# Graph layer, edge sum: the repeated operands of the one-hots move from SBUF to two PSUM banks, in runs of 8, and the tables hold each value twice

## The chip, the core and the metric

One core of a Trainium2 chip runs the whole kernel. The metric is the device time of one execution in microseconds (us), lower is better. The kernel before takes 2285.66 us, the median of 3 runs (2284.79 to 2289.71).

## What is computed

`x` holds 6250 nodes of 256 numbers. There are 200,000 edges with random `src`, `dst` and weight; the reference sorts them by `dst`, but its graph sum reads them as a sparse matrix whose row is `src` and whose column is `dst`.

```
out = segment_sum(edge_weight[:, None] * xn[dst], src, 6250) + node_vec1      # the edge sum
x = x + out + linear_attention(xn)                                            # xn = layernorm(x)
x = x + mixture_of_8_experts_top_2(layernorm(x))
```

Only the first line, the edge sum, is touched by the change.

## The kernel before, in words

The kernel runs in stages: `front` (layer norm, keys and values), `edge_sum`, `stragglers` (edges that did not fit), `route` and `experts`. The change lies in `edge_sum`.

`edge_sum` cuts the nodes into 49 blocks of 128 and works on 7 groups of source blocks (`NG = 7`), each with all 49 target tiles: 343 **steps**, in 49 **units** of 7 steps (`BU = 7`). All of it is written out straight, engine by engine; the order on each engine is that of its function `unit`, and the engines meet through semaphores alone.

A step `t` needs the edges between one group and one tile. They lie in a **table**, one row of 23 small numbers for each of 128 slots (3 of the column `PICK`, 4 each of source, target and three parts of a weight). A step goes like this:

- DVE, `hots` (lines 1278 to 1290): it compares `ends` with the values of the slot, each repeated along the free axis, and so makes the one-hots `hot` (1408 elements of bf16). Then it multiplies the one-hots of the source by the three parts of the weight into `hot_w` (1536 elements of bf16). `picks` (line 1295) makes `pick_w` (384 elements of f32) in the same way from `hot` and the f32 weights.
- PE, `blocks` (L903): 12 matmuls of bf16 make a 128 x 512 block of weights in bank 0 or 1.
- ACT, `evacuate` (L1027) copies the block to SBUF (`stage`).
- PE, `rows` (L911, L915): 8 matmuls of f32 with the window of `xn` and 6 with the rows that POOL gathered (L817, three indirect DMAs a step into four sets of buffers).
- DVE, `add` (L1316) adds the sum to `acc`.

The repeated operands are `cur` (bf16, each value of a table row repeated `REP = 16` times) and `cur_w` (f32, likewise). ACT writes them once per unit for the 7 steps of the next unit, in `take` (L1019 and L1021), in two halves of 4 and 3 steps, into one of two buffers in turn. DVE reads each run of 16 eight times over (128 / `REP`).

In the first 42 units the engines also sort the edges of a later group, one sort a unit. PE adds 34 short matmuls `base` (L845, in the first step of a unit) and 34 of `make_table` (L854, in the last). DVE adds the instructions L1121 to L1186, the large ones 816 to 2176 elements wide. ACT adds copies that repeat operands (L973, L981, L996) and `unpack` or `unpack_list` (L1002, L1007, L1010), which move the finished column of a table from PSUM into `table[par]`. There DVE splits the bit fields in place: `part` (L1172, L1173) in one unit, `make_list` (L1180 to L1186) in the next, in turn. Eight sorts run ahead of the first step (`AHEAD`), beside the matmuls `mix` (L864) of the attention, which use the banks `mix_ps`. The last 7 units sort nothing and normalise rows for the next stage instead.

The buffers bound how far an engine runs ahead: DVE makes the one-hots of step `t + i + 2` in its iteration `i` and ends the iteration with the sum of step `t + i - 1`; PE makes the blocks of step `t + i + 1` in its iteration `i` and then the rows of `t + i`.

Of the kernel before, what the change touches and what calls it, by code (L numbers as in the profile page):

```python
# [22 lines left out]
P = 128  # L23
F32 = mybir.dt.float32
# [12 lines left out]
REP = 16  # L37
SREP = 16
BU = 7
NB = 49  # L40
# [575 lines left out]
def edge_sum(nc, shared, edges, mixing, hot_w, xn_dram, xT_dram, base_dram, sum_dram, z_dram, Wg, bg, bias, wg, gb_row, G, NG, NT, N, D, HD):  # L616
# [22 lines left out]
    with ExitStack() as ctx:  # L639
# [19 lines left out]
        table = [sb(f"table{i}", [P, NB, ROWS], BF16) for i in range(2)]  # L659
# [7 lines left out]
        cur = [sb(f"cur{i}", [P, BU, ROWS, REP], BF16) for i in range(2)]  # L667
        cur_w = [sb(f"cur_w{i}", [P, BU, PICK, REP]) for i in range(2)]
# [5 lines left out]
        block_sb = [stage[:, DENSE * D + i * DENSE * P:DENSE * D + (i + 1) * DENSE * P].rearrange("p (j c) -> p j c", c=P) for i in range(2)]  # L674

# [26 lines left out]
        mix_ps = [banks[i][:, 0:D] for i in range(4)]  # L702
# [251 lines left out]
        def _(act):  # L954
# [43 lines left out]
            def unpack(s, j, par):  # L998

                act.wait_ge(table_made, s + 1)  # L1000
                at = table[par][:, :, AT_SRC:ROWS].rearrange("p b (f j) -> p b f j", j=DENSE)
                act.copy(at[:, :, :, bass.ds(j, 1)].rearrange("p b f a -> p (f a) b"), table_ps).then_inc(unpacked, 1)  # L1002

            def unpack_list(s, n, q, par):

                act.wait_ge(table_made, s + 1)
                act.copy(table[par][:, :, bass.ds(q, 1)].rearrange("p b a -> p (a b)"), table_ps[:, END, :])  # L1007
                if later(n):
                    act.wait_ge(listed, 3 * n)
                act.copy(raw[:, :, :], table_ps).then_inc(unpacked, 1)  # L1010

            def take(t, odd, par, k, half):


                act.wait_ge(w_done, t + 1)
                a, b = ((0, 4), (4, BU))[half]
                if half == 0:
                    act.wait_ge(pick_done, t + 1)
                    act.copy(cur_w[odd][:, :, :, :].rearrange("p i q r -> p (i q) r"),  # L1019
                             weight[par][:, bass.ds(k * BU, BU), :].rearrange("p i q -> p (i q)").unsqueeze(2).broadcast_to([P, BU * PICK, REP]))  # L1020
                act.copy(cur[odd][:, a:b, :, :].rearrange("p i f r -> p (i f) r"),  # L1021
                         table[par][:, bass.ds(k * BU + a, b - a), :].rearrange("p i f -> p (i f)").unsqueeze(2).broadcast_to([P, (b - a) * ROWS, REP])).then_inc(cur_done, 1)
# [18 lines left out]
            def begin():  # L1041
# [3 lines left out]
                take(0, 0, 0, 0, 0)  # L1045
                take(0, 0, 0, 0, 1)
                evacuate(0, 0)

            def unit(g, k, odd, par, turn, more, after, q):
# [4 lines left out]
                for i in range(BU):  # L1054
# [18 lines left out]
                    if after and i in (2, 4):  # L1073
                        if turned:
# [3 lines left out]
                            take(t, 1 - odd, 1 - par, 0, i // 2 - 1)  # L1078
                        else:
                            take(t, 1 - odd, par, k + 1, i // 2 - 1)  # L1080
# [20 lines left out]
        def _(dve):  # L1101
# [65 lines left out]
            def part(s, j, par):  # L1167

                dve.wait_ge(unpacked, s + 1)
                bits = table[par][:, :, :].bitcast(U16)  # L1170
                both, dst = (bits[:, :, at:at + DENSE][:, :, bass.ds(j, 1)].rearrange("p b a -> p (a b)") for at in (AT_SRC, PICK))
# [3 lines left out]
            def make_list(s, n, q, par):  # L1175
# [3 lines left out]
                col = table[par][:, :, :].bitcast(U16)[:, :, bass.ds(q, 1)].rearrange("p b a -> p (a b)")  # L1179
# [98 lines left out]
            def hots(t, i, odd, free):  # L1278

                if free is not None:  # L1280
                    dve.wait_ge(a_done, free)
                of = cur[odd]
# [3 lines left out]
                                  of[:, i, 0:HOTS, :].unsqueeze(2).broadcast_to([P, HOTS, RUNS, REP]), ALU.is_equal).then_inc(hot_done, 1)  # L1286
# [3 lines left out]
                                  of[:, i, HOTS:ROWS, :].rearrange("p (f g) r -> p f g r", f=PARTS).unsqueeze(3).broadcast_to([P, PARTS, DENSE, RUNS, REP]), ALU.mult).then_inc(w_done, 1)  # L1290

            def picks(t, i, odd):
# [823 lines left out]
```

## Time and profile before

| | before |
|---|---|
| time, median of 3 runs (without profile) | 2285.66 us (2284.79 to 2289.71) |
| span of the profiled execution, first to last instruction | 2536.7 us |
| mean granted TensorE clock in it | 0.929 |
| busy share of the span | PE 88%, weight loads 76%, DVE 77%, POOL 61%, ACT 46% |
| edge sum with sorts, units | 42, about 35.8 us each in the profile |
| edge sum without sorts, units | 7, about 34 us each in the profile |

The span is all that is shown of the profiled execution's own time: what lies around it (start and end of the program) is in no row, and the span alone is 251 us longer than the median of the runs without profile. Durations of single instructions are read from the profile; the length of the whole is measured on the runs without it. A clock of 1.0 is 2.4 GHz, of 0.5 is 1.2 GHz.

### The profile page before, as it was taken

To read this page: it belongs to the slowest core of one execution; us is meant where nothing else is said; L and a number is where in the kernel's file an instruction comes from. 1 tells how busy PE (TensorE), PEld (TensorE's weight loads), DVE (VectorE), ACT (ScalarE), POOL (GpSimd) and SP (SyncE) were. 2 spreads that over 40 slices of the span, in tenths; PEclk is the share of its full clock that TensorE was granted. 3 is DMA by queue.
4 is the path that set the end of the run, shared out by engine and by line. 5 is a ranking of instruction groups with operands and counts; after the bars stand their busy time and mean duration, and the time that the engine had idled before them with its cause. 6 is when DMAs were issued, how large, how long until landed. Compare 5 with 4: busy or idle time off the path is not lost. (4 is left out here: it accounts for less than half of the span.)

```text
span 2536.7 us, 45539 instructions
## 1 busy us (share of the span) xinstructions
PE 2230.1 (88%) x16549; PEld 1930.5 (76%) x16550; DVE 1963.9 (77%) x3350; ACT 1174.3 (46%) x1696; POOL 1551.1 (61%) x1356
## 2 busy tenths in 40 slices
PE   7987799999999899989988998999989944999993
PEld 4656687777887788778877787778877844999993
DVE  7989888788898788878877897879877757555552
ACT  2236544443444344434443454444322235888772
POOL 4750266666676566666665666666766612778883
PEclk9989999999999899989988999999999977999997
DMA  5532422222223222222222222222244453455555
GB/s 151 150 113 87 123 82 75 76 90 78 74 83 90 73 82 76 88 76 80 76 82 73 83 79 84 78 79 77 82 123 139 136 180 61 79 81 83 82 81 133
DMA packets 160931, 235.90 MB, mean 93 GB/s; under 512 B 54834, under 2 KB 121805, under 8 KB 160490
## 3 DMA queue, kind: packets, MB, share of 16 engines
q0 software_dynamic: 70896, 164.43, 25.4%
q1 hardware_dynamic: 75536, 55.29, 7.9%
q10 hardware_dynamic: 14314, 13.68, 1.6%
q8 instruction: 120, 1.97, 0.3%
q14 instruction: 65, 0.53, 0.1%
HBM read 186.46 MB, written 53.24 MB: 94 GB/s over the span
## 5 line engine op out<-in xcount | busy, mean ns | idle before, releaser
L817 POOL DMA_INDIRECT picked<-xn_dram,place x1029 | 1143.9, 1112 | 721.7 <-PE bank L915 289.8
L1027 ACT COPY stage<-bank 128x512 f32<-128x512 f32 x343 | 201.0, 586 | 796.9 <-remote 477.6
L915 PE MATMUL bank<-picked,pick_w 128*128 128x256 f32 x2058 | 518.4, 389 | 3.3 <-issue 3.3
L915 PEld LDWEIGHTS bank<-picked,pick_w 128*128 128x128 f32 x2058 | 405.7, 197 | 65.8 <-issue 5.2
L911 PE MATMUL bank<-window,stage 128*128 128x256 f32 x1568 | 416.9, 409 | 17.8 <-issue 12.8
L903 PE MATMUL bank<-hot_w,hots 128*128 128x128 bf16 x4116 | 312.0, 225 | 49.1 <-issue 44.8
L911 PEld LDWEIGHTS bank<-window,stage 128*128 128x128 f32 x1568 | 300.4, 202 | 65.1 <-issue 25.6
L1164 DVE TENSOR_TENSOR vals<-hot_t,field_rep 128x1666 bf16<-128x1666 bf16 x200 | 203.7, 1041 | 187.8 <-remote 180.2
L1288 DVE TENSOR_TENSOR hot_w<-hots,cur 128x1536 bf16<-128x1536 bf16 x343 | 328.6, 958 | 11.9
L903 PEld LDWEIGHTS bank<-hot_w,hots 128*128 128x128 bf16 x4116 | 267.1, 101 | 92.5 <-issue 54.5
L911 PE MATMUL bank<-stage 128*128 128x256 f32 x1176 | 315.5, 410 | 11.6 <-issue 10.4
L981 ACT COPY field_rep<-fields 128x1666 bf16<-128x1666 bf16 (+1 forms) x193 | 322.8, 1677 | 1.2 <-DVE vals L1164 1.2
L1284 DVE TENSOR_TENSOR hots<-ends,cur 128x1408 bf16<-128x1408 bf16 x343 | 303.1, 884 | 1.7 <-ACT cur L1021 1.7
L911 PEld LDWEIGHTS bank<-stage 128*128 128x128 f32 x1176 | 225.9, 203 | 49.0 <-issue 23.2
L1908 POOL DMA_INDIRECT sum_dram<-y,target x112 | 179.1, 1599 | 64.0 <-issue 31.1
L1316 DVE TENSOR_TENSOR acc<-acc,bank 128x256 f32<-128x256 f32 x343 | 142.3, 415 | 85.2 <-PE bank L915 44.7
L1295 DVE TENSOR_TENSOR pick_w<-hots,cur_w 128x384 f32<-128x384 bf16 x343 | 190.6, 556 | 0.2
L1899 POOL DMA_INDIRECT zin<-z_dram,token x112 | 115.5, 1031 | 83.4 <-POOLq L1600 49.6
L2002 PE MATMUL bank<-w,hh 128*128 x896 | 163.6, 282 | 1.1 <-DVE hl L2050 1.1
L854 PE MATMUL bank<-vals,slot 128*128 128x196 bf16 x1700 | 155.8, 249 | 4.9 <-issue 4.0
L854 PEld LDWEIGHTS bank<-vals,slot 128*128 128x128 bf16 x1700 | 147.9, 98 | 12.3 <-issue 5.8
L2002 PEld LDWEIGHTS bank<-w,hh 128*128 128x128 f32 x896 | 138.2, 189 | 1.4 <-issue 1.4
(253 smaller groups left out, 3414.6 us busy)
## 6 DMA issues: line engine op xcount, KB each, us to landing
picked<-xn_dram,place POOLq DMA_INDIRECT x1029
w<-in_L_ffn_W_dram SPq DMA_DIRECT2D x16, 512.0 KB, 8.9
xn_dram<-xn ACTq DMA_DIRECT2D x49, 128.0 KB, 1.9
xT_dram<-xT ACTq DMA_DIRECT2D x49, 128.0 KB, 2.1
base_dram<-acc SPq DMA_DIRECT2D x7, 896.0 KB
sum_dram<-acc SPq DMA_DIRECT2D x7, 896.0 KB
z_dram<-vals SPq DMA_DIRECT2D x7, 896.0 KB
out_dram<-sum_dram SPq DMA_DIRECT2D x1, 6250.0 KB, 21.8
```

The costliest lines, as they stand in the source:

```text
L817: pool.indirect_dma_start(out=picked[:, i % SETS * PICK + q, :], out_offset=None, in_=xn_dram, in_offset=bass.IndirectOffsetOnAxis(ap=plac ...
L854: mm = pe.matmul(table_ps, slot[:, c, :], vals[:, c, :, :], start=(c == 0), stop=(c == CH - 1))
L903: mm = pe.matmul(block_ps(pp, j), hot[buf][:, PICK + j, :], hot_w[buf][:, part, j, :], start=(part == 0), stop=(part == 2))
L911: pe.matmul(sum_ps[pp], block_sb[pp][:, j, :], window[par][:, j, :], start=(j == 0), stop=False)
L915: mm = pe.matmul(sum_ps[pp], pick_w[i % SETS][:, q, :], picked[:, i % SETS * PICK + q, :], start=False, stop=(q == PICK - 1))
L981: act.copy(field_rep[:, :, a:b, :], fields[:, a:b, bass.ds(s, 1), :].rearrange("p f a c -> p (a c) f").unsqueeze(3).broadcast_to([P, CH, b ...
L1027: act.copy(block_sb[pp].rearrange("p j c -> p (j c)"), banks[pp][:, :]).then_inc(a_copied, 1)
L1164: ins = dve.tensor_tensor(vals[:, :, f, :], hot_t[:, :, :], field_rep[:, :, f, :], ALU.mult)
L1284: dve.tensor_tensor(to[:, :, :].rearrange("p f (b r) -> p f b r", r=REP), ends[:, :, :].rearrange("p f (b r) -> p f b r", r=REP), of[:, i, ...
L1288: dve.tensor_tensor(hot_w[i % SETS][:, :, :, :].rearrange("p f g (b r) -> p f g b r", r=REP), to[:, AT_SRC:HOTS, :].rearrange("p g (b r) - ...
L1295: dve.tensor_tensor(pick_w[i % SETS][:, :, :].rearrange("p q (b r) -> p q b r", r=REP), hot[i % SETS][:, 0:PICK, :].rearrange("p q (b r) - ...
L2002: mm = pe.matmul(y_ps[i][:, n * D:(n + 1) * D], parts[a][:, c, n * P:(n + 1) * P], w, start=(m == 0), stop=(m == 3 * FC - 1))
```

## The change

Three things are done together.

1. `cur` and `cur_w` leave SBUF. The operands of steps 0 to 3 of a unit live in PSUM bank 2, those of steps 4 to 6 in bank 3. There is one buffer for each half in place of two for the whole unit, so ACT takes a half after the last step that reads it: half 0 in iteration 3 (before: 2), half 1 in iteration 6 (before: 4). Each take now carries its own part of the weights, and both wait for `w_done` and `pick_done`.
2. Runs are 8 long (`REP = 8`), and DVE reads each 16 times over. A half of 4 steps takes 368 words of pairs of bf16 and 96 of f32, of the 512 that a bank has.
3. The tables change from `[block, row]` to `[row, block, 2]`: each value of bf16 stands there twice. ACT moves a pair as one f32 word, so `take` copies 368 + 96 and 276 + 72 elements where it copied 1472 + 336 and 1104. `unpack` writes 392 elements in runs that touch (before: 196, spread out), `unpack_list` 98 (before: 49), and `part` and `make_list` work on 98 touching elements of 16 bits in place of 49 spread ones.

The banks of `mix` before the first step are 0, 1, 4 and 5 in place of 0 to 3. The number of instructions of DVE and PE stays, and their order; ACT has one more in each unit.

```diff
-REP = 16
+REP = 8
...
-        table = [sb(f"table{i}", [P, NB, ROWS], BF16) for i in range(2)]
+        table = [sb(f"table{i}", [P, ROWS, NB, 2], BF16) for i in range(2)]
...
-        cur = [sb(f"cur{i}", [P, BU, ROWS, REP], BF16) for i in range(2)]
-        cur_w = [sb(f"cur_w{i}", [P, BU, PICK, REP]) for i in range(2)]
...
+        CUT = (0, 4, BU)
+        CUR_W = CUT[1] * ROWS * (REP // 2)
...
+        def cur_words(half):
+            return banks[2 + half][:, 0:(CUT[half + 1] - CUT[half]) * ROWS * (REP // 2)]
+        def cur_w(half):
+            return banks[2 + half][:, CUR_W:CUR_W + (CUT[half + 1] - CUT[half]) * PICK * REP]
+        def cur_of(i):
+            half = 0 if i < CUT[1] else 1
+            return cur_words(half).bitcast(BF16).rearrange("p (i f r) -> p i f r", f=ROWS, r=REP)[:, i - CUT[half], :, :]
...
-        mix_ps = [banks[i][:, 0:D] for i in range(4)]
+        mix_ps = [banks[i][:, 0:D] for i in (0, 1, 4, 5)]
...
-            def take(t, odd, par, k, half):
-                act.wait_ge(w_done, t + 1)
-                a, b = ((0, 4), (4, BU))[half]
-                if half == 0:
-                    act.wait_ge(pick_done, t + 1)
-                    act.copy(cur_w[odd] ... weight[par] ... broadcast_to([P, BU * PICK, REP]))
-                act.copy(cur[odd][:, a:b, :, :] ... table[par] ... broadcast_to([P, (b - a) * ROWS, REP])).then_inc(cur_done, 1)
+            def take(used, par, k, half):
+                act.wait_ge(w_done, used + 1)
+                act.wait_ge(pick_done, used + 1)
+                a, n = k * BU + CUT[half], CUT[half + 1] - CUT[half]
+                act.copy(cur_w(half) ... weight[par] ... broadcast_to([P, n * PICK, REP]))
+                words = table[par][:, :, :, :].rearrange("p f b h -> p (f b h)").bitcast(F32).rearrange("p (f b) -> p b f", b=NB)
+                act.copy(cur_words(half) ... words[:, a:a + n, :] ... broadcast_to([P, n, ROWS, REP // 2])).then_inc(cur_done, 1)
...
-                    if after and i in (2, 4):
+                    if after and i in (CUT[1] - 1, CUT[2] - 1):
...
-                            take(t, 1 - odd, par, k + 1, i // 2 - 1)
+                            take(t + i + 1, par, k + 1, i // CUT[1])
...
-                of = cur[odd]
+                of = cur_of(i)
...
-                                  of[:, i, 0:HOTS, :].unsqueeze(2).broadcast_to([P, HOTS, RUNS, REP]), ALU.is_equal).then_inc(hot_done, 1)
+                                  of[:, 0:HOTS, :].unsqueeze(2).broadcast_to([P, HOTS, RUNS, REP]), ALU.is_equal).then_inc(hot_done, 1)
```

On ACT, in the first unit of the edge sum, this stands before (L1019 and L1021 are the take, L1027 the evacuation of a block):

```order
L1027 COPY stage<-bank 128x512 [waits o_done,a_done]
L1019 COPY cur_w<-weights 128x336 [waits pick_done,w_done]
L1021 COPY cur<-table 128x1472
L1027 COPY stage<-bank 128x512 [waits o_done,a_done]
L981 COPY field_rep<-fields 128x34x49 [waits vals_done]
L1027 COPY stage<-bank 128x512 [waits o_done,a_done]
L1021 COPY cur<-table 128x1104 [waits w_done]
L996 COPY rank_rep<-rank 128x544 [waits ranked,slot_done]
```

and this in the changed kernel (L1038 and L1041 are the take, L1047 the evacuation):

```order
L1047 COPY stage<-bank 128x512 [waits o_done,a_done] x2
L1038 COPY bank<-weights 128x96 [waits pick_done,w_done]
L1041 COPY bank<-table 128x368
L1001 COPY field_rep<-fields 128x34x49 [waits vals_done]
L1047 COPY stage<-bank 128x512 [waits o_done,a_done]
L1016 COPY rank_rep<-rank 128x544 [waits ranked,slot_done]
L1047 COPY stage<-bank 128x512 [waits o_done,a_done]
L993 COPY tile_rep<-tile 128x1666 [waits same_done,tiles_done]
L994 COPY tile_pad<-tile 128x34
L995 COPY tile_pad<-tile 128x34
L1047 COPY stage<-bank 128x512 [waits o_done,a_done]
L1038 COPY bank<-weights 128x72 [waits pick_done,w_done]
```

The first take stands one evacuation later, the second two, and both are short.

On DVE nothing moves; the operand changes its place. At the first steps of the edge sum stood, before:

```order
L1284 TENSOR_TENSOR hots<-ends,cur 128x1408 [waits cur_done]
L1288 TENSOR_TENSOR hot_w<-hots,cur 128x1536 [waits hot_done]
L1295 TENSOR_TENSOR pick_w<-hots,cur_w 128x384 [waits hot_done]
L1284 TENSOR_TENSOR hots<-ends,cur 128x1408
L1288 TENSOR_TENSOR hot_w<-hots,cur 128x1536 [waits hot_done]
```

and in the changed kernel:

```order
L1303 TENSOR_TENSOR hots<-ends,bank 128x1408 [waits cur_done]
L1307 TENSOR_TENSOR hot_w<-hots,bank 128x1536 [waits hot_done]
L1314 TENSOR_TENSOR pick_w<-hots,bank 128x384 [waits hot_done]
L1303 TENSOR_TENSOR hots<-ends,bank 128x1408
L1307 TENSOR_TENSOR hot_w<-hots,bank 128x1536 [waits hot_done]
```

The second input of all three is now a bank.

## Rows read from the trace of the kernel before

**Rows 1.** The page: span and busy shares
```profile
span 2536.7 us, 45539 instructions
...
PE 2230.1 (88%) x16549; PEld 1930.5 (76%) x16550; DVE 1963.9 (77%) x3350; ACT 1174.3 (46%) x1696; POOL 1551.1 (61%) x1356
```

**Rows 2.** DVE in order of time: start us, duration us, instruction, [idle before]
```profile
422.55 0.77 DVE L1125 TENSOR_TENSOR same<-tile_pad,tile_rep 128x1156 bf16<-128x1156 bf16 x1
...
674.67 0.77 DVE L1125 TENSOR_TENSOR same<-tile_pad,tile_rep 128x1156 bf16<-128x1156 bf16 x1
...
705.10 2.00 DVE L1164 TENSOR_TENSOR vals<-hot_t,field_rep 128x1666 bf16<-128x1666 bf16 x2 [4.44 <-remote]
...
709.84 0.77 DVE L1125 TENSOR_TENSOR same<-tile_pad,tile_rep 128x1156 bf16<-128x1156 bf16 x1
...
733.19 0.42 DVE L1316 TENSOR_TENSOR acc<-acc,bank 128x256 f32<-128x256 f32 x1 [0.94 <-PE bank L915]
...
740.29 0.77 DVE L1125 TENSOR_TENSOR same<-tile_pad,tile_rep 128x1156 bf16<-128x1156 bf16 x1
...
1784.62 0.77 DVE L1125 TENSOR_TENSOR same<-tile_pad,tile_rep 128x1156 bf16<-128x1156 bf16 x1
```

**Rows 3.** PE in order of time, same columns, in the unit from 712 us
```profile
712.88 0.83 PE L903 MATMUL bank<-hot_w,hots 128*128 128x128 bf16 x12
...
731.62 3.06 PE L854 MATMUL bank<-vals,slot 128*128 128x196 bf16 x34
...
734.52 0.83 PE L903 MATMUL bank<-hot_w,hots 128*128 128x128 bf16 x12
...
738.26 1.16 PE L845 MATMUL bank<-hot_t,before 128*128 128x49 bf16 x34
...
739.26 0.22 PE L903 MATMUL bank<-hot_w,hots 128*128 128x128 bf16 x1
```

**Rows 4.** Groups of DVE by shape, 420 to 1790 us: busy us, mean ns | idle before
```profile
L1288 DVE TENSOR_TENSOR hot_w<-hots,cur 128x1536 bf16<-128x1536 bf16 x268 | 256.8, 958 | 9.3
L1284 DVE TENSOR_TENSOR hots<-ends,cur 128x1408 bf16<-128x1408 bf16 x268 | 236.9, 884 | 0.0
L1164 DVE TENSOR_TENSOR vals<-hot_t,field_rep 128x1666 bf16<-128x1666 bf16 x153 | 156.0, 1042 | 176.0 <-remote 169.0 <-issue 6.6 <-PE bank L854 0.4
L1295 DVE TENSOR_TENSOR pick_w<-hots,cur_w 128x384 f32<-128x384 bf16 x268 | 149.2, 557 | 0.0
L1316 DVE TENSOR_TENSOR acc<-acc,bank 128x256 f32<-128x256 f32 x268 | 111.0, 414 | 15.7 <-PE bank L915 8.6 <-remote 6.6 <-issue 0.2
L1153 DVE TENSOR_TENSOR slot<-iota_j,rank_rep 128x2176 bf16<-128x2176 bf16 x76 | 94.5, 1285 | 0.0
...
L1180 DVE TENSOR_SCALAR table<-table 128x49 uint16<-128x49 uint16 x17 | 4.6, 270 | 0.0
```

**Rows 5.** Groups by shape, whole span: a DVE product with an operand in PSUM
```profile
L2034 DVE TENSOR_TENSOR zl<-bank,zh 128x512 fp32r<-128x512 f32 x56 | 38.0, 678 | 8.4 <-ACT zh L1923 4.5 <-issue 3.8
```

**Rows 6.** Groups of ACT by shape, 420 to 1790 us, same columns
```profile
L1021 ACT COPY cur<-table 128x1472 bf16<-128x1472 bf16 x38 | 54.3, 1428 | 0.0
L1021 ACT COPY cur<-table 128x1104 bf16<-128x1104 bf16 x38 | 42.3, 1114 | 0.0
```

**Rows 7.** POOL and DVE in order of time, columns as in rows 2
```profile
733.42 0.94 POOL L817 DMA_INDIRECT picked<-xn_dram,place  x1 [1.39 <-PE bank L915]
...
739.37 1.49 POOL L817 DMA_INDIRECT picked<-xn_dram,place  x1 [0.30 <-issue]
...
739.08 0.96 DVE L1288 TENSOR_TENSOR hot_w<-hots,cur 128x1536 bf16<-128x1536 bf16 x1
```

**Rows 8.** All engines at the first step of the edge sum
```profile
297.80 0.47 ACT L1019 COPY cur_w<-weights 128x336 f32<-128x336 f32 x1 [3.79 <-DVE table L1173]
...
300.64 0.89 DVE L1284 TENSOR_TENSOR hots<-ends,cur 128x1408 bf16<-128x1408 bf16 x1 [1.66 <-ACT cur L1021]
```

**Rows 9.** Stretches: from:to, length, busy us of each engine; 1800 to 2040 us
```profile
1800.00:2040.00 240.00, 219.50 (x1508) 191.48 (x1506) 178.56 (x334) 62.60 (x115) 163.04 (x147) 0.96 0.43 123
```

More of the change, by code:

```diff
@@ L1010, in unpack_list @@
                 act.copy(raw[:, :, :], table_ps).then_inc(unpacked, 1)
-            def take(t, odd, par, k, half):
-                act.wait_ge(w_done, t + 1)
-                a, b = ((0, 4), (4, BU))[half]
-                if half == 0:
-                    act.wait_ge(pick_done, t + 1)
[L1019 to L1022, printed above, removed]
+            def take(used, par, k, half):
+                act.wait_ge(w_done, used + 1)
+                act.wait_ge(pick_done, used + 1)
+                a, n = k * BU + CUT[half], CUT[half + 1] - CUT[half]
+                act.copy(cur_w(half).rearrange("p (m r) -> p m r", r=REP),
+                         weight[par][:, a:a + n, :].rearrange("p i q -> p (i q)").unsqueeze(2).broadcast_to([P, n * PICK, REP]))
+                words = table[par][:, :, :, :].rearrange("p f b h -> p (f b h)").bitcast(F32).rearrange("p (f b) -> p b f", b=NB)
+                act.copy(cur_words(half).rearrange("p (i f r) -> p i f r", f=ROWS, r=REP // 2),
+                         words[:, a:a + n, :].unsqueeze(3).broadcast_to([P, n, ROWS, REP // 2])).then_inc(cur_done, 1)
             def evacuate(t, pp):
@@ L1044, in begin @@
                 act.wait_ge(listed, 3 * PICK)
-                take(0, 0, 0, 0, 0)
-                take(0, 0, 0, 0, 1)
+                take(0, 0, 0, 0)
+                take(0, 0, 0, 1)
                 evacuate(0, 0)
@@ L1169, in part @@
                 dve.wait_ge(unpacked, s + 1)
-                bits = table[par][:, :, :].bitcast(U16)
-                both, dst = (bits[:, :, at:at + DENSE][:, :, bass.ds(j, 1)].rearrange("p b a -> p (a b)") for at in (AT_SRC, PICK))
+                both, dst = (table[par][:, at + j, :, :].rearrange("p b h -> p (b h)").bitcast(U16) for at in (AT_SRC, PICK))
                 dve.tensor_scalar(dst, both, 0x7F80, None, ALU.bitwise_and)
@@ L1276, in sort, with hots @@
                     make_list(s - 1, s // 2 - 1, s // 2 - 1, 0)
-            def hots(t, i, odd, free):
+            def hots(t, i, free):
                 if free is not None:
                     dve.wait_ge(a_done, free)
-                of = cur[odd]
+                of = cur_of(i)
                 to = hot[i % SETS]
@@ L1302, in begin @@
                 dve.wait_ge(cur_done, 2)
-                hots(0, 0, 0, None)
-                picks(0, 0, 0)
-                hots(1, 1, 0, None)
+                hots(0, 0, None)
+                picks(0, 0)
+                hots(1, 1, None)
                 dve.wait_ge(saved, 16 * GRP)
@@ L1323, in unit @@
                     if i + 1 < BU:
[L1324 removed]
+                        picks(t + i + 1, i + 1)
                     elif after:
[L1326 removed]
+                        picks(t + BU, 0)
                     if i == 2:
@@ L1329, in unit @@
                     if i + 2 < BU:
-                        hots(t + i + 2, i + 2, odd, t + i + 2 if i + 2 < 3 else t + i + 1)
+                        hots(t + i + 2, i + 2, t + i + 2 if i + 2 < 3 else t + i + 1)
                     elif after:
@@ L1333, in unit @@
                             dve.wait_ge(cur_done, 2 * (u + 1) + 1)
-                        hots(t + i + 2, i + 2 - BU, 1 - odd, t + i + 2)
+                        hots(t + i + 2, i + 2 - BU, t + i + 2)
                     if i > 0:
```

22 lines of the change are left out of this document (12 added, 10 removed).

## The prediction

> **What bounds the kernel now.** I read the page first. PE is busy for 88% of the span, DVE for 77%, ACT for 46% [rows 1]: two engines are near full. Then the order of time in the edge sum, where the change lies. One DVE instruction, L1125, stands once in each unit, so the distance of two of them is a unit: 38 units from 422.55 to 1784.62 us make 35.84 us each [rows 2]. But a unit is not full. The unit from 674.67 to 709.84 holds one idle stretch of 4.44 us in front of L1164, "remote", that is, no semaphore event that the trace shows ended it; over 38 units that line sat idle for 176 us [rows 2, 4]. The unit from 709.84 to 740.29 has no such hole: 30.45 us, of which 0.94 is a wait for PE [rows 2]. So DVE has 35.17 - 4.44 = 30.7 us of work in a unit of the one kind (with the list) and 29.5 in one of the other (with the parts), 30.1 on average.
>
> Now PE in the same unit. From the blocks at 712.88 to the table at 731.62 it works off 5 steps without a gap, 3.748 us each; the table takes 2.90 us and the base 1.00 [rows 3]. 7 x 3.748 + 2.90 + 1.00 = 30.1 us. **PE and DVE are equally full**, at 30.1 us a unit.
>
> The runs without profile are 251 us shorter than this span alone [rows 1]. 42 units at 35.84 instead of some 30.3 account for (35.84 - 30.3) x 42 = 233 us of it. I take from this that the holes belong to the profiled execution and that a timed unit lasts 30.1 to 30.4: 30.1 if the engines' buffers smooth the two kinds of unit fully, (30.7 + 30.1) / 2 = 30.4 if not at all. My sum is made against the profiled execution's 2536.7 us for the durations, but its terms count only where PE or DVE works without a hole, and I apply it to the median of the runs, 2285.7 us; the same difference should show in the span, give or take what the holes do.
>
> **The change, part by part.**
>
> *The DVE products with an operand in PSUM* (21 a unit, 343 of each in all). This decides. Before, both inputs are in SBUF. `hots` 1408 elements in 884 ns and `slot` 2176 in 1285 ns give (1285 - 884) / 768 = 0.52 ns an element and 149 ns fixed [rows 4]. Rows with an operand in PSUM exist only for f32: `acc`, 256 elements in 414 ns, and `zl`, 512 in 678 ns, give 1.03 ns an element and 150 ns fixed [rows 4, 5]. `pick_w` with both in SBUF, f32, takes 557 ns for 384: 1.03 x 384 + 161. So reading PSUM costs nothing fixed here, and nothing for f32. The Trainium skill says otherwise of the fixed part: page "VectorE: DVE Perf Modes", section "The TRN2 errata", has 58 cycles from SBUF and 120 from PSUM. At its 0.96 GHz that would be an estimated 65 ns an instruction, 1.4 us a unit and some +44 us in all; the trace does not agree, with 149 ns beside 150. What no row shows is a bf16 operand in PSUM. Bounds: at the rate of the bf16 rows the change is 0 (no gain: 0.52 ns is the best that any product here shows, and the fixed part is equal). At the rate of the PSUM rows, +0.51 x 1408 = +0.72 us for `hots` and +0.51 x 1536 = +0.78 us for `hot_w`, 1.50 us a step, 10.5 us a unit. I take 0, because in the rows the rate goes with the width of the elements (f32 in SBUF runs at the same 1.03 as f32 in PSUM), not with the memory.
>
> *Runs of 8 instead of 16.* `hots` has 176 runs instead of 88, `hot_w` 192 instead of 96, `pick_w` 48 instead of 24. The nearest rows: `vals` with rows of 49 has 1042 - 0.52 x 1666 = 176 ns fixed, 27 more than `hots` and `slot`, over 34 breaks, 0.8 ns a break [rows 4]; but `slot`, with runs of 16, shows none. Bounds 0 and 0.8 x (88 + 96 + 24) = 0.17 us a step, 1.2 us a unit. I take 0, by the rows with repeated runs, which are of the same kind.
>
> *The copies of ACT.* 1472 elements take 1428 ns and 1104 take 1114: 0.853 ns an element, 172 ns fixed [rows 6]. 368 and 276 words come to about 0.49 and 0.41 us, so some 1.6 us of ACT work go from each unit. ACT is busy 46% of the span [rows 1] and this work lies beside PE's. Its new place: half 0 is written in ACT's iteration 3 and first read in DVE's iteration 5, half 1 in iteration 6 and read in iteration 2 of the next unit. That is two iterations or more of at least 3.75 us [rows 3] for about 0.8 us of copies. What queues behind the copies on ACT is the next evacuation, for which PE waits; it comes after one more step. The new waits (`w_done`, `pick_done` of the last reader) ask for products that stand on DVE ahead of the one-hots from which PE made the block that ACT has just evacuated, so they are met when ACT gets there. I cost this at 0. If the cover went, the price would be a copy a unit, under 1 us.
>
> Only the first take is on the path: it starts at 297.80 and DVE's first `hots` at 300.64 [rows 8]. With 812 words in place of 2912, 2100 x 0.853 = 1.8 us less, and one more instruction of about 0.1: **-1.7 us**, once.
>
> *The tables.* 77 small in-place instructions of DVE (270 ns for 49 spread elements [rows 4]) get 98 that touch. Bounds: twice the elements at 1.03 ns, +0.05 us, or the spread was what cost, -0.05 us each; at two a part unit and one a list unit, +-0.07 us a unit, +-3 us in all. I take **-1**. ACT's unpacking is shorter or longer by under half a microsecond, far from the path. The other banks of `mix` have the same rotation of four: 0.
>
> *POOL.* At 733.42, beside `acc`, which has an operand in PSUM, a gather takes 0.94 us; at 739.37, started 0.29 us into `hot_w`, which has none, 1.49 us: 0.55 more, about what was left of `hot_w` [rows 7]. So the gathers beside the three products should fall to 0.94 us. But POOL waits for PE within that unit (1.39 us at 733.42), so it was not late, and I count 0. The Trainium skill states such a rule (page "SBUF — State Buffer", section "Who interferes with whom"): a DVE instruction with two SBUF inputs contends with a GpSimd instruction that reads SBUF. By that, the trace agrees for `hot_w`.
>
> Sum: -1.7 - 1 = -2.7. **Forecast 2283 us**, and a difference of about 0.2% (4.6 us) is what a measurement of this kernel can tell from none.
>
> **The rivals.**
>
> *Forecast: DVE's rate holds, PE sets the pace, nothing much happens.* Chance 0.38. Own range 2278 to 2289, from the terms above and the table's bounds.
>
> *A. The relief reaches the path.* In the runs without holes POOL has less lead than the trace shows: 21 gathers at 1.11 + 0.30 us make 29.6 us a unit, near PE's 30.1. If its stretched gathers, or DVE's uneven units, hold PE now, a unit falls from 30.4 to PE's 30.1: 42 x 0.3 = 12.6 us, with the start 14: 2271. If the 251 - 233 = 18 us that I could not place were also edge sum, up to 2255. Against: PE waits for no gather in the rows read. Chance 0.34.
>
> *B. The short runs cost.* Half to all of the 1.2 us a unit lands on an engine that is already full: DVE has 30.1 + 1.2 = 31.3 us against 30.4 now, +0.9 x 42 = +38 us at the full price, 2321; about 2300 at half. It decides from the point where DVE's average passes what a unit lasts now, 0.3 us a unit, 14 ns an instruction: that little. Chance 0.16.
>
> *C. The products with a bf16 operand in PSUM run at 1.03 ns an element* (slower, and the place is DVE in every step). 30.1 + 10.5 = 40.6 us a unit against 30.4: 42 x 10.2 = +428 us. In the last 7 units DVE works 179 of 240 us [rows 9], 26 of 34 a unit, and 36.5 with this: +2.5 x 7 = +17. Together 2730. For it: every row with a PSUM operand runs at that. Against: all of them are f32, and f32 does so in SBUF too. The Trainium skill speaks on both sides: page "VectorE: DVE Perf Modes", section "The perf-mode tier table (the rule you actually need)", gives `tensor_tensor` with any PSUM operand one element a cycle, while its section "Why PSUM operands drop a tier" still allows two for 16-bit elements. No row here shows which. Chance 0.12.
>
> That the change does not do what it says I exclude: on DVE the second input of all three products is a bank, and the ACT copies have the stated widths.
>
> **How the numbers follow.** The predicted time is the likeliest case's, 2283. The range runs from 2264 (A, up to half of its far end) to 2322 (B at full price), and leaves out C (0.12) and some 0.05 at the ends. Faster by over 0.2%, under 2281.1: A, 0.34. Within 0.2%: the forecast, 0.38. Slower: B and C, 0.28.
>
> **What would show it.** Right: `hots` at 0.88, `hot_w` at 0.96 and `pick_w` at 0.56 us with a bank as input; the ACT take at about 0.5 and 0.4 us; PE steps at 3.75 us and no wait of PE for ACT or DVE that was not there; gathers started within `hot_w` at 0.94. `hots` at 1.6 us means C, `hots` between 0.90 and 0.97 means B. The forecast is wrong if PE's pitch itself changes, or if the DVE rate holds and the time still moves by over 0.5%: then a timed unit is not bound as I read it from the unit without a hole.

## The result, and the profile after

The changed kernel takes 2258.28 us, the median of 4 runs (2257.62 to 2259.40). The kernel before takes 2287.26 us beside it (2284.79 to 2289.71, 4 runs). The ratio is 0.987, with a 95% interval of 0.9856 to 0.9884: 29 us, or 1.3%, faster. Forecast was 2283, range 2264 to 2322.

The chips on which the kernels ran are of two kinds. On three of them every version took 2514 to 2704 us (medians), and its traces show idle stretches in the edge sum that no semaphore explains. On the others every version took 2258 to 2348 us, and the traces show no such stretches. By its span (2536.7 [rows 1]) and its stretches the trace of before that stands ahead of the prediction belongs to the first kind; the times beside it, and the times and the trace of the changed kernel in this section, belong to the second. Each chip was used on one occasion only, so whether the kind stays with a chip is not shown. Each experiment below is therefore compared with the kernel before on the same chip, and the changed kernel's trace with that of a run of the kernel before without stretches (`e1_before_again`).

The page of the changed kernel: span, busy shares, and POOL's group of gathers with its idle time.

```profile
span 2255.8 us, 45631 instructions
...
PE 2091.7 (93%) x16549; PEld 1854.7 (82%) x16550; DVE 1950.6 (86%) x3350; ACT 1079.5 (48%) x1745; POOL 1455.2 (65%) x1356
...
L837 POOL DMA_INDIRECT picked<-xn_dram,place x1029 | 1048.1, 1019 | 538.4 <-issue 283.6
```

DVE in the order of time (start, duration), answering to [rows 2] and [rows 8]: the first one-hots of the edge sum, then the first and the last mark of the 41 units between them.

```profile
298.98 0.87 DVE L1303 TENSOR_TENSOR hots<-ends,bank 128x1408 bf16<-128x1408 bf16 x1
...
311.01 0.77 DVE L1145 TENSOR_TENSOR same<-tile_pad,tile_rep 128x1156 bf16<-128x1156 bf16 x1
...
1539.56 0.79 DVE L1145 TENSOR_TENSOR same<-tile_pad,tile_rep 128x1156 bf16<-128x1156 bf16 x1
```

A unit lasts (1539.56 - 311.01) / 41 = 29.96 us. DVE's first one-hots are early by the forecast 1.7 us (298.98 against 300.64).

The groups of DVE by shape, 420 to 1500 us, answering to [rows 4] (busy us, mean ns | idle before):

```profile
L1307 DVE TENSOR_TENSOR hot_w<-hots,bank 128x1536 bf16<-128x1536 bf16 x253 | 241.3, 954 | 8.7
L1303 DVE TENSOR_TENSOR hots<-ends,bank 128x1408 bf16<-128x1408 bf16 x253 | 222.4, 879 | 0.0
L1184 DVE TENSOR_TENSOR vals<-hot_t,field_rep 128x1666 bf16<-128x1666 bf16 x144 | 148.1, 1051 | 5.8 <-PE bank L874 5.8
L1314 DVE TENSOR_TENSOR pick_w<-hots,bank 128x384 f32<-128x384 bf16 x252 | 137.4, 545 | 0.0
...
L1199 DVE TENSOR_SCALAR table<-table 128x98 uint16<-128x98 uint16 x15 | 4.1, 274 | 0.0
L1191 DVE TENSOR_SCALAR table<-table 128x98 uint16<-128x98 uint16 x21 | 3.9, 185 | 0.0
```

With an operand in a bank the three products take 954, 879 and 545 ns, where they took 958, 884 and 557. The 176 us in front of `vals` [rows 4] are gone.

ACT's groups, 460 to 1500 us, answering to [rows 6]:

```profile
L1041 ACT COPY bank<-table 128x368 f32<-128x368 f32 x35 | 16.6, 473 | 0.0
L1041 ACT COPY bank<-table 128x276 f32<-128x276 f32 x35 | 13.9, 397 | 0.0
```

POOL's gathers in the same stretch, by group and then by what they waited for (us in total, times, longest; 320 to 1530 us):

```profile
L837 POOL DMA_INDIRECT picked<-xn_dram,place x729 | 747.0, 1025 | 294.2 <-issue 202.6 <-PE bank L935 91.7
```

```profile
POOL picked L837 <- issue: 234.3, 769, 0.3
...
POOL picked L837 <- PE bank L935: 109.1, 75, 4.3
```

A gather takes 1025 ns on average, and 0.30 us ("issue", in which POOL waits for nothing that the profile shows) stands before each; POOL is ahead and waits for PE. And how they stand beside DVE, in the order of time, answering to [rows 7]:

```profile
1118.16 0.95 POOL L837 DMA_INDIRECT picked<-xn_dram,place  x1 [0.30 <-issue]
...
1120.66 1.33 POOL L837 DMA_INDIRECT picked<-xn_dram,place  x1 [0.30 <-issue]
```

```profile
1118.04 0.95 DVE L1307 TENSOR_TENSOR hot_w<-hots,bank 128x1536 bf16<-128x1536 bf16 x1
...
1120.14 1.03 DVE L1154 TENSOR_TENSOR earlier<-hot_t,base_sb 128x1666 bf16<-128x1666 bf16 x1
```

Within `hot_w`, which now reads a bank, a gather takes 0.95 us (1.49 at [rows 7]). Beside a sort instruction that still reads two tiles of SBUF it takes 1.33. From 320 to 1530 us PE is busy for 1209.98 of 1210 us: it never stops.

### The profile page after: what moved, and what is told of

The parts are those of the page before. It is cut to its first block and busy times, and to the rows that moved or that the text cites. A ratio compares the mean times of both kernels' runs of the same rounds, so it can differ in the third digit from the quotient of the medians.

```text
span 2255.8 us, 45631 instructions
## 1 busy us (share of the span) xinstructions
PE 2091.7 (93%) x16549; PEld 1854.7 (82%) x16550; DVE 1950.6 (86%) x3350; ACT 1079.5 (48%) x1745; POOL 1455.2 (65%) x1356
## 5 line engine op out<-in xcount | busy, mean ns | idle before, releaser
L837 POOL DMA_INDIRECT picked<-xn_dram,place x1029 | 1048.1, 1019 | 538.4 <-issue 283.6
L935 PE MATMUL bank<-picked,pick_w 128*128 128x256 f32 x2058 | 500.1, 379 | 0.0
L1047 ACT COPY stage<-bank 128x512 f32<-128x512 f32 x343 | 200.9, 586 | 599.6 <-PE bank L923 593.8
L935 PEld LDWEIGHTS bank<-picked,pick_w 128*128 128x128 f32 x2058 | 391.0, 190 | 53.2
L931 PE MATMUL bank<-window,stage 128*128 128x256 f32 x1568 | 381.4, 386 | 0.0
L1307 DVE TENSOR_TENSOR hot_w<-hots,bank 128x1536 bf16<-128x1536 bf16 x343 | 327.2, 954 | 11.8
L931 PEld LDWEIGHTS bank<-window,stage 128*128 128x128 f32 x1568 | 282.6, 190 | 30.3
L1303 DVE TENSOR_TENSOR hots<-ends,bank 128x1408 bf16<-128x1408 bf16 x343 | 301.5, 879 | 0.0
L923 PE MATMUL bank<-hot_w,hots 128*128 128x128 bf16 x4116 | 285.6, 219 | 2.4 <-DVE hot_w L1307 2.0
L931 PE MATMUL bank<-stage 128*128 128x256 f32 x1176 | 286.0, 386 | 0.0
L1927 POOL DMA_INDIRECT sum_dram<-y,target x112 | 179.2, 1600 | 62.2 <-issue 30.1
L1314 DVE TENSOR_TENSOR pick_w<-hots,bank 128x384 f32<-128x384 bf16 x343 | 187.0, 545 | 1.2 <-DMA base_dram<-acc 1.0
L1335 DVE TENSOR_TENSOR acc<-acc,bank 128x256 f32<-128x256 f32 x343 | 142.1, 414 | 34.2 <-PE bank L935 34.2
```

Of the source, the lines that this page charges most:

```text
L837: pool.indirect_dma_start(out=picked[:, i % SETS * PICK + q, :], out_offset=None, in_=xn_dram, in_offset=bass.IndirectOffsetOnAxis(ap=plac ...
L923: mm = pe.matmul(block_ps(pp, j), hot[buf][:, PICK + j, :], hot_w[buf][:, part, j, :], start=(part == 0), stop=(part == 2))
L931: pe.matmul(sum_ps[pp], block_sb[pp][:, j, :], window[par][:, j, :], start=(j == 0), stop=False)
L935: mm = pe.matmul(sum_ps[pp], pick_w[i % SETS][:, q, :], picked[:, i % SETS * PICK + q, :], start=False, stop=(q == PICK - 1))
L1047: act.copy(block_sb[pp].rearrange("p j c -> p (j c)"), banks[pp][:, :]).then_inc(a_copied, 1)
L1303: dve.tensor_tensor(to[:, :, :].rearrange("p f (b r) -> p f b r", r=REP), ends[:, :, :].rearrange("p f (b r) -> p f b r", r=REP), of[:, 0: ...
```

## The experiments

The rivals after the result were: the memory of the operands relieves POOL (theory **M**); the shorter runs, the pairs or the lighter ACT do it (**R**); or the 29 us are the stretches.

### The kernel before, without stretches

No edit.

> The kernel before, unchanged, for a second trace. If the idle stretches in front of L1164 (4 to 8 us in most units, none in the changed kernel's trace) belong to the profiled execution alone, they need not come back, and a unit then shows what the timed runs have: 2287 us means 42 units of about 30.65 us if all of the 29 us lies there. Theory POOL (its stretched gathers hold PE): PE waits at L915 for DMA, or POOL never waits for PE. Theory DVE (PE and DVE uneven): DVE shows no idle time in the list units and PE waits for hot_w. Theory ACT (the 1.9 us of copies in one piece delay an evacuation): PE waits at L911 for stage. If the holes come back with a time of 2287 outside the profile, they are an effect of profiling.

Measured: 2291.79 us (one run), span 2290.0. Marks of the units on DVE, and the last sum of the edge sum:

```profile
311.57 0.77 DVE L1125 TENSOR_TENSOR same<-tile_pad,tile_rep 128x1156 bf16<-128x1156 bf16 x1
...
1566.16 0.77 DVE L1125 TENSOR_TENSOR same<-tile_pad,tile_rep 128x1156 bf16<-128x1156 bf16 x1
...
1808.17 0.42 DVE L1316 TENSOR_TENSOR acc<-acc,bank 128x256 f32<-128x256 f32 x1 [2.49 <-PE bank L915]
```

(1566.16 - 311.57) / 41 = 30.60 us a unit, 0.64 more than after the change. The first five last 29.4 to 30.3 us, as in the changed kernel; from the sixth on they go up to 31.8. The last eight units (one with a sort, seven without) differ too. From the last mark to the last sum they take 1808.17 - 1566.16 = 242.0 us here, and in the changed kernel 1772.81 - 1539.56 = 233.3:

```profile
1772.81 0.42 DVE L1335 TENSOR_TENSOR acc<-acc,bank 128x256 f32<-128x256 f32 x1 [2.49 <-PE bank L935]
```

The group of gathers, 460 to 1500 us, and then the waits of 320 to 1560 us:

```profile
L817 POOL DMA_INDIRECT picked<-xn_dram,place x712 | 824.8, 1158 | 216.9 <-issue 210.6 <-PE bank L915 6.4
```

```profile
POOL picked L817 <- issue: 248.9, 817, 0.3
...
PEld bank L915 <- issue: 32.0, 51, 1.4
DVE acc L1316 <- PE bank L915: 17.4, 19, 1.2
PE bank L915 <- DMA picked<-xn_dram,place: 14.4, 27, 1.0
```

The POOL row is the case. Busy and idle make 824.8 + 216.9 = 1041.7 us in a stretch of 1040: POOL does nothing else than gather, it waits for PE 6.4 us in all of it, and 21 gathers of 1.158 + 0.30 us make 30.6 us, which is the unit. PE then waits for gathered rows, as in this row of PE in the order of time:

```profile
826.10 1.53 PE L915 MATMUL bank<-picked,pick_w 128*128 128x256 f32 x6 [0.84 <-DMA picked<-xn_dram,place]
```

PE is busy for 1224.91 of 1240 us here. Its recorded waits are at the gathered rows (L915). Its weight loads waited for DVE twice, 1.1 us in all, which speaks against theory DVE, and nothing waited for `stage`, which theory ACT asked for. The waits of weight loads and of matmuls are recorded apart and add up to less than what the units lose between the marks; how they overlap the profile doesn't show.

In the units without sorts POOL is nearly full as well: from 1600 to 1700 us it works for 75.40 us on 71 gathers, which with 0.30 each makes 96.7 of 100 us, and PE is busy for 93.87. In the changed kernel 71 gathers take 66.79 us there, and PE is busy all the time. In the eight units PE stands still for 6.8 us before the change and for 1.2 after it, which is 5.6 of the 8.8 us.

Why a gather takes 1.158 us, from POOL and DVE at one place:

```profile
1093.72 1.49 POOL L817 DMA_INDIRECT picked<-xn_dram,place  x1 [0.30 <-issue]
```

```profile
1093.44 0.96 DVE L1288 TENSOR_TENSOR hot_w<-hots,cur 128x1536 bf16<-128x1536 bf16 x1
```

The gather ends at 1095.21, 0.81 us after the end of `hot_w`. All 105 gathers of 460 to 1500 us that began within `hot_w` end 0.81 to 0.83 us after it and take 1.48 to 1.50; of the 140 that began in `pick_w`, 104 again end 0.81 to 0.83 after it (up to 1.32 us each), and the 36 that began in its first 0.03 us take the plain 0.95. In the changed kernel the 71 in `hot_w`, 116 in `pick_w` and 158 in `hots` all take 0.94 to 0.96.

### All of the change but the memory, and the runs of 8 alone

```diff
+        half_sb = [sb(f"half{i}", [P, 512]) for i in range(2)]
...
-            return banks[2 + half][:, 0:(CUT[half + 1] - CUT[half]) * ROWS * (REP // 2)]
+            return half_sb[half][:, 0:(CUT[half + 1] - CUT[half]) * ROWS * (REP // 2)]
...
-            return banks[2 + half][:, CUR_W:CUR_W + (CUT[half + 1] - CUT[half]) * PICK * REP]
+            return half_sb[half][:, CUR_W:CUR_W + (CUT[half + 1] - CUT[half]) * PICK * REP]
```

> The changed kernel, but the two halves of the repeated operands lie in SBUF tiles of the same size, everything else as changed (runs of 8, pairs, one buffer a half, late takes). It parts the memory from the rest. Theory POOL: gathers that start within hots, hot_w or pick_w are stretched again (1.1 us on average instead of 1.02) and the time goes back to about 2280 to 2287. Theories DVE and ACT: the time stays at 2258 to 2262, since the copies and the small instructions keep their gain.

Measured: 2288.09 us (2281.65 to 2291.83), ratio 0.9997 (0.9982 to 1.0011). Groups of DVE and POOL, 460 to 1500 us:

```profile
L1308 DVE TENSOR_TENSOR hot_w<-hots,half 128x1536 bf16<-128x1536 bf16 x237 | 227.0, 958 | 8.2
L1304 DVE TENSOR_TENSOR hots<-ends,half 128x1408 bf16<-128x1408 bf16 x237 | 209.0, 882 | 0.0
```

```profile
L838 POOL DMA_INDIRECT picked<-xn_dram,place x713 | 823.9, 1156 | 217.3 <-issue 209.7 <-PE bank L936 7.6
```

With pairs, late takes, short copies and runs of 8, but tiles in SBUF, POOL is as full as before and nothing is gained. Without the memory there is no gain, and theory R falls.

The kernel before with shorter runs:

```diff
-REP = 16
+REP = 8
```

> The kernel before with runs of 8 instead of 16, in SBUF, nothing else. ACT's copies for a unit fall from 2912 to 1456 elements (3.0 to 1.7 us). Theory ACT: most of the 29 us comes, 2258 to 2268. Theory POOL and theory DVE: 2282 to 2290. If short runs cost DVE in SBUF, hots is over 0.90 us and the time over 2300.

Measured: 2286.56 us (2282.09 to 2290.98), ratio 1.0001 (0.9987 to 1.0014). `hots` takes 882 ns and `pick_w` 556: 88 more breaks cost nothing. ACT's copies of `cur` fall from about 1419 and 1114 to 806 and 654 ns, and that gains nothing either. Its traced run took 2284.51 us, with units of 30.37 us and 244.4 us for the last eight, so with both inputs in SBUF a unit lasts 30.4 to 30.6 us from one run to another.

### Less for POOL

The kernel before, without the third gather of a step from step 8 on:

```diff
+        def gathers(t):
+            return PICK if t < BU else PICK - 1
...
-                for q in range(PICK):
+                for q in range(gathers(t)):
```

> The kernel before, but from the eighth step on POOL gathers two of the three blocks of rows a step (the third is left out, its matmul reads old rows), so POOL has a third less to do and everything else is as before. Theory POOL: with POOL far from full, the time falls to 2258 or below. Theories DVE and ACT: 2280 to 2289.

Measured: 2258.44 us (2256.84 to 2259.37), ratio 0.9877 (0.9853 to 0.9900). A repeat on another chip without stretches:

> As e4, the kernel before with two gathers a step from the eighth step on (the third is left out). On a chip without the idle stretches it repeats 2258. On a chip with them it asks what they hang on: in the traces they stand behind the dense short matmuls (base, make_table) in units with gathers, but not in the eight sorts ahead, which have the same matmuls and no gathers. If they come from both together, a third fewer gathers shortens them: below 2450 where the kernel before takes 2535 to 2549. If they come from the matmuls alone, the time stays within 1% of the kernel before.

Measured: 2258.22 us, ratio 0.9878 (0.9857 to 0.9900). This chip had no stretches, so the question what they hang on got no answer. The stretch of 460 to 1500 us of the first (length; busy us of PE, PEld, DVE, ACT, POOL; clock; DMA share; GB/s):

```profile
460.00:1500.00 1040.00, 1040.00 (x8659) 929.80 (x8655) 1024.23 (x1504) 553.90 (x710) 561.73 (x485) 1.00 0.22 65
```

With a third of the gathers gone and DVE's operands still in SBUF, the time is that of the changed kernel to a fraction of a microsecond, and PE is busy in all of the stretch. A gather still takes 1160 ns, but 14 x 1.46 = 20.4 us are far below 30. So POOL's sum was the bound before, and the 29.97 us that a unit lasts here is the next one, PE's with DVE close behind (1024 of 1040).

### More for POOL

The changed kernel with three more gathers in a unit, into a spare tile that nobody reads:

```diff
+            EXTRA, more = (1, 3, 5), [0]
...
+                if i in EXTRA and t >= BU:
+                    if more[0]:
+                        pool.wait_ge(spare_in, 16 * more[0])
+                    more[0] += 1
+                    pool.indirect_dma_start(out=spare[:, :], out_offset=None, in_=xn_dram,
+                                            in_offset=bass.IndirectOffsetOnAxis(ap=place[g % 2][:, 0, b:b + 1], axis=0)).then_inc(spare_in, 16)
```

> As e15. On a chip without the idle stretches, theory POOL: 24 x 1.32 = 31.7 us a unit, 1.7 over 29.96, 41 units: 2315 to 2335, with PE waiting for DMA at the gathered rows; if POOL's sum did not count: 2258. With the stretches: ratio about 1.06, as e15.

Measured: 2347.95 us (2346.30 to 2350.64), ratio 1.0274 (1.0250 to 1.0298) against the kernel before: more than I expected. The gathers of 460 to 1500 us, then the waits:

```profile
L840 POOL DMA_INDIRECT picked<-xn_dram,place x678 | 694.0, 1024 | 206.6 <-issue 199.3 <-PE bank L945 7.3
L846 POOL DMA_INDIRECT more_rows<-xn_dram,place x98 | 110.8, 1130 | 29.9 <-issue 29.6 <-PE bank L945 0.3
```

```profile
PEld bank L945 <- issue: 75.8, 75, 2.7
DVE acc L1345 <- PE bank L945: 59.4, 29, 2.7
PE bank L945 <- DMA picked<-xn_dram,place: 49.2, 50, 2.3
```

POOL's sum is 21 x 1.324 + 3 x 1.43 = 32.1 us, and a unit lasts 32.0 (marks at 309.29 and 1623.11, 41 units). (32.04 - 29.96) x 41 = 85 of the 90 us over the changed kernel, and the last eight units, 8 us longer (241.3), are the most of the rest. My expectation had 31.7 us for that sum and nothing for the last eight. The waits that the kernel before had are back, larger. With 20.4, 27.8, 30.6 and 32.1 us of POOL work a unit lasts 29.97, 29.96, 30.60 and 32.0: it follows the larger of POOL and PE.

### Which of the three operands

The changed kernel with the bf16 values (for `hots` and `hot_w`) in SBUF and only the f32 weights (for `pick_w`) in the bank:

```diff
-            return banks[2 + half][:, 0:(CUT[half + 1] - CUT[half]) * ROWS * (REP // 2)]
+            return half_sb[half][:, 0:(CUT[half + 1] - CUT[half]) * ROWS * (REP // 2)]
```

> As e13: only the bf16 values of the halves back in SBUF. On a chip without the idle stretches, theory POOL: the mean gather goes from 1.02 to about 1.12 us, 21 x 1.42 = 29.8 us a unit against PE's 30.0, so most of the gain stays: 2262 to 2278. With them: ratio 0.99 to 1.00, as e11 and e13.

Measured: 2262.33 us (2259.49 to 2263.35), ratio 0.9890 (0.9870 to 0.9910), at the lower edge of what I expected. POOL, 460 to 1500 us:

```profile
L838 POOL DMA_INDIRECT picked<-xn_dram,place x728 | 791.4, 1087 | 249.5 <-issue 203.0 <-PE bank L936 46.5
```

58 gathers within `hot_w` still take 1.64 us on average, but the 123 in `pick_w` take 0.95, and 21 x (1.087 + 0.30) = 29.1 us is below 29.96. The marks of this trace are 29.97 us apart, as in the changed kernel, and PE is busy for all of the 1040 us. The 4 us that it is slower lie in the last eight units: 237.7 us, between 233.3 and 242.0. In the units with sorts it is a threshold and not a proportion: half of the relief already gives the whole gain there, and 24 of the 29 us in all. It also speaks against a rival of the expectations further down, that every stretched gather costs: with these still stretched, a unit with a sort is no longer than in the changed kernel.

### The chips with stretches

The same variants were also run there. Their edits are those above; "weights in SBUF" is the mirror of the last one (of the two lines that `e2_halves_in_sbuf` changed, only that of `CUR_W`), and "one gather more" has `EXTRA = (3,)`. On the first such chip (before: 2535.37 us) the expectations were written for a chip without stretches. As numbers all four missed, and the runs don't test POOL's sum:

> The changed kernel with only the f32 weights (the operand of pick_w, 384 elements) back in SBUF; hots and hot_w keep their operand in PSUM. Theory POOL (what counts is what POOL needs for 21 gathers a unit against the 30.0 us that PE needs): gathers that start in hots or hot_w stay at 0.95 us, those that start in pick_w wait up to 0.35 us more; the mean goes from 1.02 to about 1.05 us, 21 x 1.35 = 28.4 us a unit, under 30.0: 2258 to 2261. Rival (any stretched gather costs, because each delays rows that PE needs soon): 2264 or more.

Measured: 2527.21 us, ratio 0.9989 (0.9960 to 1.0018).

> The changed kernel with only the bf16 values (the operand of hots and hot_w) back in SBUF; the weights stay in PSUM. Theory POOL: most of the stretching comes back (a gather started 0.3 us into hot_w takes 1.49 us), the mean is about 1.12 us, 21 x 1.42 = 29.8 us a unit, at the edge of PE's 30.0: 2262 to 2278. If the time is 2285 or more, the threshold lies below what I take; if it is 2259 or less, pick_w did the harm.

Measured: 2513.91 us, ratio 0.9921 (0.9877 to 0.9965).

> The changed kernel with one gather more a unit (the first of step 3 again, into a spare tile that nobody reads), 22 in place of 21. Theory POOL: 22 x 1.32 = 29.0 us a unit is still under 30.0: 2257 to 2261. Rival (POOL's latency counts, not its sum): 2264 or more.

Measured: 2594.73 us, ratio 1.0269 (1.0210 to 1.0328).

> The changed kernel with three gathers more a unit (steps 1, 3 and 5), 24 in place of 21. Theory POOL: 24 x 1.32 = 31.7 us a unit, 1.7 over the present 29.96, in 41 units with sorts: +70 us, 2315 to 2335, with PE waiting for DMA at the gathered rows. If the sum of POOL's work didn't matter, 2258.

Measured: 2667.97 us, ratio 1.0545 (1.0495 to 1.0595).

On the second (before: 2532.78 us):

> The changed kernel as it is, beside the kernel before on one chip. The chip of e5 to e8 ran the kernel before in 2535 us, with the idle stretches in front of the sort's vals that my first trace had; the chip of e1 to e4 in 2288 us, without them. If this is a chip without the stretches: 2258, ratio 0.987. If it has them: theory POOL says that POOL gets a rest in every stretch and is never short, so the change gives next to nothing, ratio 0.99 to 1.00.

Measured: 2554.54 us (2538.92 to 2567.01), ratio 1.0113 (1.0074 to 1.0152): here the change is **slower**, by 22 us, where I had expected 0.99 to 1.00. The waits, 460 to 1500 us:

```profile
POOL picked L837 <- PE bank L935: 264.1, 90, 8.8
ACT stage L1047 <- PE bank L923: 261.9, 115, 10.8
ACT stage L1047 <- remote: 228.3, 42, 11.5
```

POOL waits for PE for a quarter of the time, in the stretches, so its sum is not the bound there and the relief has nothing to give. That explains a ratio of 1.00, but not the 22 us.

> As e5: only the f32 weights back in SBUF. On a chip without the idle stretches, theory POOL: mean gather about 1.05 us, 21 x 1.35 = 28.4 us a unit, under PE's 30.0: 2258 to 2261. Rival (every stretched gather costs): 2264 or more. On a chip with them: like e5, within 0.5% of the kernel before.

Measured: 2557.31 us, ratio 1.0108 (1.0030 to 1.0187), not within the 0.5% that I expected.

> As e6: only the bf16 values back in SBUF. On a chip without the idle stretches, theory POOL: mean gather about 1.12 us, 21 x 1.42 = 29.8 us a unit, at the edge of PE's 30.0: 2262 to 2278.

Measured: 2532.47 us, ratio 1.0011 (0.9970 to 1.0052).

> As e8: three gathers more a unit, 24 in place of 21, in the changed kernel. On a chip without the idle stretches, theory POOL: 24 x 1.32 = 31.7 us a unit, 1.7 over 29.96, 41 units: 2315 to 2335. If POOL's sum did not count: 2258.

Measured: 2703.56 us, ratio 1.0694 (1.0619 to 1.0770).

On the third (before: 2548.50 us):

> As e11, for a chip without the idle stretches (kernel before at 2288): only the bf16 values back in SBUF. Theory POOL: mean gather about 1.12 us, 21 x 1.42 = 29.8 us a unit, at the edge of PE's 30.0: 2262 to 2278. If the kernel before takes some 2535 us, the stretches are there and the run only repeats e11 (ratio 0.99 to 1.005).

Measured: 2523.23 us, ratio 0.9889 (0.9845 to 0.9934).

> As e10, for a chip without the idle stretches: only the f32 weights back in SBUF. Theory POOL: 21 x 1.35 = 28.4 us a unit, under PE's 30.0: 2258 to 2261. Rival (every stretched gather costs): 2264 or more. With the stretches: ratio about 1.01, as e10.

Measured: 2564.30 us, ratio 1.0056 (1.0024 to 1.0087).

> As e12, for a chip without the idle stretches: 24 gathers a unit in the changed kernel. Theory POOL: 24 x 1.32 = 31.7 us a unit, 1.7 over 29.96, 41 units: 2315 to 2335. If POOL's sum did not count: 2258. With the stretches: ratio about 1.07, as e12.

Measured: 2695.54 us, ratio 1.0584 (1.0548 to 1.0620).

What follows from these eleven runs is less than I wanted. Three more gathers a unit cost 149 us over the changed kernel on the second chip, where POOL has time to spare, against 90 on a chip without stretches: the stretches grow with the gathers, and do not come from POOL being late.

Where they begin can be read, though. PE's waits of 460 to 1500 us in the trace of the kernel before that stands ahead of the prediction:

```profile
PE bank L845 <- issue: 43.0, 56, 1.2
PE bank L903 <- issue: 23.7, 40, 1.8
PE bank L911 <- issue: 15.0, 22, 1.6
```

It is PE that stands still, for nothing that the profile shows, most of all within the 34 short matmuls `base`; DVE, ACT and POOL then wait behind it. PE is busy for 952.80 of the 1040 us at a mean granted clock of 0.94, against 1040.00 at 1.00 in the changed kernel without stretches. The changed kernel on the second chip has 934.99 at 0.93, and with three gathers more 899.23 at 0.90. In the stretch in front of L1164 at 705.10 the clock was 1.00 while PE stood still, and was 0.50 (1.2 GHz) from 707 to 710 us, behind it.

On each of the three chips the version with the values in SBUF is 13 to 41 us faster than the one with the weights in SBUF. Why PE stands still stays open, and so does why the bf16 values in a bank cost something there. Weights in SBUF was never run on a chip without stretches. The version with only the weights in the bank is 24, 21, 0 and 25 us faster than the kernel before on four chips, so it is the one that never lost; without stretches the change as made is faster by another 4 us (2258.28 against 2262.33, on different chips).

## Why the prediction was wrong, and where it was right

The forecast case, "DVE's rate holds, PE sets the pace, nothing much happens", had the DVE rate and PE's own sum right, but PE did not set the pace before the change: it gave -0.1%, and -1.3% was measured. What happened is rival A, by its own mechanism (stretched gathers hold PE). That the time lies at its far end (2255, measured 2258) is luck: that end added 18 us which I could not place, and what the runs showed in its place is 0.64 us a unit where I had 0.3, and 9 us in the last eight units.

- **POOL: "it was not late, and I count 0": this step failed.** It rested on one wait of 1.39 us for PE [rows 7] and on a mean of 1.11 us a gather. Both came from a trace with stretches, in which POOL works on while the others stand still: of 609 gathers from 460 to 1500 us 68 began within `hot_w` and 117 beside no DVE instruction at all, against 105 and 37 of 712 without stretches. There a gather takes 1.158 + 0.30 us and POOL has no slack: 30.6 us a unit, above PE's 30.1 that I had worked out. Relieved, 27.8. In rival A I had 29.6 for POOL and 0.3 us a unit for the gain, half of what it was. By the two traces the term is 1254.6 - 1228.6 = 26.0 us over the 41 units between the marks and 8.8 us in the last eight units, which I had not counted at all; the first take leaves 0.6 us at the first mark, and behind the edge sum the changed kernel loses 1.2. That makes the 34.2 us between the two spans (2290.0 and 2255.8); the traced run of before was 4.5 us above its median, and the medians are 29 us apart.
- **PE's 30.1 us a unit: right.** Once POOL is relieved, a unit lasts 29.96 us, and 29.97 in both other versions in which POOL is not short.
- **"The holes belong to the profiled execution": failed too.** On three chips the runs without a profile are as long as those with one (2535.37, 2532.78 and 2548.50 us for the kernel before), so the lost time is there without the profiler too. This is the root of the first error: a span 11% over the median of the runs is not a profile of those runs. I then discounted the holes in PE's and DVE's sums but read POOL's slack from the same trace as it stood.
- **The products with a bf16 operand in PSUM: right**, and it excludes rival C. 879 and 954 ns are no slower than from SBUF, so the rate did go with the width of the elements. The Trainium skill (page "VectorE: DVE Perf Modes") spoke on both sides: the trace agrees with its section "Why PSUM operands drop a tier", which leaves 16-bit elements the double rate, and not with the one-a-cycle entry of "The perf-mode tier table (the rule you actually need)". Nor did the larger fixed cost from PSUM of "The TRN2 errata" show: `pick_w` is 12 ns shorter, not the estimated 65 longer.
- **Runs of 8: right at 0**, by 882 ns for `hots` in `e3_runs_of_8`. Rival B fell.
- **ACT's copies: right**, 473 and 397 ns for 0.49 and 0.41, and hidden. The first take: right, 1.7 us at its place.
- **The tables:** L1191 fell from 270 to 185 ns, outside my bound of -0.05, L1199 stayed at 274; about 0.1 us a unit in DVE's work, which is not the bound.
- **The gather beside `hot_w`: right** at 0.95 us, and so was the rule beside it (the Trainium skill, page "SBUF — State Buffer", section "Who interferes with whom": two SBUF inputs of DVE against a GpSimd instruction that reads SBUF). I had the mechanism and the size of a gather and set its effect to 0 at the last step, on a slack that was not there.

## What to carry to other kernels

Where DVE runs two-input products without a pause and POOL issues gathers beside them, put the small repeated operand in a free PSUM bank: here the product kept its rate, and the gathers lost their stretch. It pays only if POOL's own sum (duration and issue) is at or above the pitch of the engine that sets the pace, so add that sum up before costing it at 0, and stop at the operand that brings it below. Before any slack is read from a trace, hold its span against the measured times: slack from a disturbed trace is slack that the timed kernel may not have. And measure on more than one chip: where PE stood still for a reason that no trace shows, the same change cost 1.1%.

## What the runs showed of the hardware

- A gather that begins within a DVE product with two SBUF inputs is held until 0.81 to 0.83 us after that product's end (105 of 105 in `hot_w`, 1.48 to 1.50 us each; 104 of 140 in `pick_w`; 31 of 31 in `earlier` L1154 of the changed kernel, 0.81 to 0.82). Of these, the 36 that began in the first 0.03 us of `pick_w` were not held (0.95 us). Two in `earlier` (L1134) of the kernel before took 2.91 us each: the one at 742.51 us ended 0.82 us after the third such product in a row. With one input in PSUM all 345 gathers take 0.94 to 0.96 us wherever they begin.
- DVE was not held up in return: `hot_w` takes 0.96 us whether a gather began within it (105 times) or not (132 times).
- The same program takes 2285 to 2288 us on some chips and 2533 to 2549 on others, and one change has a ratio of 0.987 on one of the first and 1.011 on one of the second.
- ACT writes the repeated f32 words a little faster into PSUM than into SBUF: 473 against 500 ns for 368 (`e2_halves_in_sbuf`).
